# Moving the second convolution, the attention weights and the second Sinkhorn balancing of a fused convolution, attention and expert block

## The reference, cut to what matters

```python
x = x + _L0_conv_ref(_gn(x), ...)             # deformable convolution, 9 taps
# second layer, on g = _gn(x); x_l repeats g over n = 4 streams
x_norm = x_pooled * rsqrt(mean(x_pooled**2) + 1e-20) * rms_w
coeffs = x_norm @ phi_w.T + phi_b             # 24 numbers an image
H_pre  = sigmoid(alpha_pre * coeffs[:, :n]);  H_post = 2 * sigmoid(alpha_post * coeffs[:, n:2*n])
M = exp(alpha_res * coeffs[:, 2*n:].reshape(B, n, n))
for _ in range(20):                           # Sinkhorn: 40 half-steps
    M = M / sum(M, axis=-1, keepdims=True)
    M = M / sum(M, axis=-2, keepdims=True)
h_out = conv3x3(sum over streams of H_pre * x_l) + conv_b
x = x + mean(res_part + post_part, axis=1)    # res_part: diagonal of M times g; post_part: H_post times h_out
# third layer, on tokens t: 8 sequences of 256
t = t + attention(layernorm(t))               # 8 heads of 64, causal, softmax
# then two expert layers (8 experts top 2, 16 experts top 2) with a windowed sum between them
```

## Time and profile before

| what | value |
|---|---|
| median of 3 runs | 490.46 us |
| the profiled execution's own time | 486.73 us |
| its span, first to last instruction | 484.9 us |
| mean granted clock of TensorE | 0.982 |
| busy PE, DVE, ACT, POOL | 434.6, 347.4, 283.1, 175.6 us |
| end of the tap loop, last interpolation | 106.0 us |
| first exponential of attention | 139.05 us |
| first masks of steps 7, 16, 24, 33 | 154.89, 174.67, 194.13, 218.15 us |

### The profile page before, as it was taken

The page is one execution under the profiler, slowest core; times in us unless marked ns, Lnnn a source line. Parts: engine busy times, 40 slices in busy tenths (PEclk is TensorE's granted clock), DMA queues, the critical chain, the costliest instruction groups (busy, mean ns, idle before and its releaser), DMA issues.

```text
span 484.9 us, 9115 instructions
## 1 busy us (share of the span) xinstructions
PE 434.6 (90%) x2998; PEld 303.3 (63%) x2998; DVE 347.4 (72%) x1090; ACT 283.1 (58%) x676; POOL 175.6 (36%) x305
## 2 busy tenths in 40 slices
PE   2999999999968988979999988999989888998994
PEld 1787777767467887979898944344435444545542
DVE  4178998867777656788978853637666888797862
ACT  3467776732557876758788855765655333343431
POOL 4400001203134563383793342415341454343342
PEclk9998999999989998989999999999999999999998
DMA  7300000000400000012300004212112213041330
GB/s 178 144 2 1 2 0 1 1 2 0 87 3 1 1 2 1 2 39 51 69 20 3 1 3 141 63 39 68 43 38 74 68 45 105 28 122 66 99 102 11
DMA packets 13567, 20.94 MB, mean 43 GB/s; under 512 B 4592, under 2 KB 6384, under 8 KB 13008
## 3 DMA queue, kind: packets, MB, share of 16 engines
q1 hardware_dynamic: 13056, 19.99, 14.4%
q10 hardware_dynamic: 464, 0.37, 0.3%
HBM read 19.62 MB, written 0.72 MB: 42 GB/s over the span
## 4 chain that ended last, share of the span: by engine, by line
PE 63%; DVE 16%; ACT 8%; issue 6%; POOL 4%; DMA 2%; POOLq 0%; DVEq 0%; SPq 0%; ACTq 0%
PE PS L2171 14%; PE PS L1871 7%; PE PS L1909 6%; PE PS L2182 5%; PE PS L2193 5%; PE PS L1930 3%; PE PS L2103 3%; PE PS L2091 2%; PE PS L1829 2%; PE PS L1998 2%; PE PS L2013 2%; PE PS L2047 2%; ACT score_arena L968 2%; DVE QL L1468 2%; DVE score_arena L1577 2%
## 5 line engine op out<-in xcount | busy, mean ns | idle before, releaser
L2171 PE MATMUL PS<-YTs,WH 64*128 64x512 f32 x192 | 77.0, 427 | 1.9 <-ACT VV L1067 1.6
L735 POOL TENSOR_TENSOR pr<-pr 128x512 f32<-128x512 f32 x39 | 50.4, 1291 | 75.9 <-DVE pr L1630 44.7
L2171 PE MATMUL PS<-YX,WH 64*128 64x512 f32 x192 | 77.2, 426 | 0.0
L968 ACT ACTIVATE score_arena<-score_arena,nmx 128x128 f32<-128x128 f32 (+1 forms) x128 | 56.9, 446 | 22.2 <-DVE nmx L1577 21.8
L1067 ACT ACTIVATE VV<-PS 128x512 f32<-128x512 f32 x64 | 35.4, 595 | 41.6 <-PE PS L2171 41.5
L1023 ACT ACTIVATE stage<-PS,wk 128x512 f32<-128x512 f32 x64 | 40.8, 684 | 22.8 <-PE PS L2171 22.7
L1743 DVE TENSOR_TENSOR stage<-VV,PS 128x512 f32<-128x512 f32 x64 | 41.8, 682 | 17.1 <-ACT VV L1067 12.5
L2171 PEld LDWEIGHTS PS<-YTs,WH 64*128 64x128 f32 x192 | 35.3, 184 | 29.6 <-ACT VV L1067 12.6
L908 ACT ACTIVATE st_mem<-PS 128x512 f32<-128x512 f32 x72 | 37.3, 612 | 18.5 <-PE PS L1909 18.5
L2103 PE MATMUL PS<-cst,score_arena 128*128 128x128 f32 x192 | 34.4, 290 | 6.6 <-ACT score_arena L968 6.1
L2091 PE MATMUL PS<-YTs,QH 128*128 128x128 f32 (+1 forms) x128 | 38.9, 328 | 0.0
(11 more groups left out here) (277 smaller groups left out, 1130.1 us busy)
## 6 DMA issues: line engine op xcount, KB each, us to landing
QH<-gate_store SPq DMA_DIRECT2D x96, 128.0 KB, 2.9
stage<-in_wexp SPq DMA_DIRECT2D x6, 512.0 KB, 5.9
wk<-in_w SPq DMA_DIRECT2D x1, 1034.0 KB, 9.8
wa<-in_wat SPq DMA_DIRECT2D x1, 768.0 KB, 8.1
out<-X SPq DMA_DIRECT2D x16, 32.0 KB, 1.9
cst<-in_consts SPq DMA_DIRECT2D x1, 483.0 KB, 6.4
wc<-in_w SPq DMA_DIRECT2D x2, 183.5 KB, 5.8
score_arena<-in_wcv SPq DMA_DIRECT2D x2, 144.0 KB, 6.2
```

The lines of the kernel that those rows point to most:

```text
L735: nc.gpsimd.tensor_tensor(acc[:, c % 2], acc[:, c % 2], weighted[:, u % 2], ALU.add).then_inc(acc_added, 1)
L968: ins = nc.scalar.activation(PR[:, s % 3, cols], MS[:, s % 3, cols], ACT.Exp, bias=nmx[:, s % 3, qt:qt + 1], scale=-1.0, accum_out=rsum[:, ...
L2171: ins = mm(PS[:, banks[i], :], w[hs, m, tiles[i] * P:(tiles[i] + 1) * P], ys[i][hs, cs], start=(k == 0), stop=(k == 2))
```

## The change

Convolution 0 runs inside the tap loop, three taps after each of the steps 33, 34 and 35. Both convolutions accumulate in banks 5 and 6, and the attention weights in banks 1 to 4, so that batch 1's coefficients (now bank 4) and the gate spreads (now bank 7) move too. After the loop stand the gate spread of batch 0, the first pass of the weights, the group means and the diagonal spread, then the second pass with the first token transposes in its middle. Convolution 1 is cut in pieces: three taps before the transposes of yA, one after them, one after the first two projections, one after `scores(0)` and the other two projections, two in step 0 and one in step 1. All 40 half-steps of batch 1 run split between POOL and DVE in steps 0 to 21, two a step; its exponential moves to step 0 on ACT, its gates to step 0 on POOL and step 2 on DVE, and the spread of its gates becomes a fill of step 4 ("gS"), with ACT's bias in step 4 and DVE's convolution adds in step 5. DVE takes the middle reciprocal after both masks. The diagonal, the token transposes of tiles 2 and 3, their layer norms and one pair of folds move two or three steps later, and in image 3's steps the six projections move to steps 28 to 31.

```diff
-DIAG_AT, XT_AT, YA_AT = 18, (20, 27), (7, 25, 38)
-DVE_HALVES = 10
-POOL_HALVES = tuple(min(40, DVE_HALVES + 2 * s - (s > 3) - (s > 4)) for s in range(19))
-MID_INVERSE, END_INVERSE = [s for s in range(17) if s != 4], [s for s in range(15) if s != 3]
+DIAG_AT, XT_AT, YA_AT = 21, (22, 29), (7, 27, 38)
+DVE_HALVES = 0
+GATES_AT = 4
+POOL_HALVES = tuple(min(40, 2 * s) for s in range(21))
+MID_INVERSE, END_INVERSE = range(2, 22), range(1, 21)
...
-    return {0: (2, 3, 4, 5, 6, 7), 3: (2, 3, 4, 5, 6, 7)}.get(a, (0, 1, 2, 3, 4, 5))
+    return {0: (2, 3, 4, 5, 6, 7), 3: (4, 5, 5, 6, 6, 7)}.get(a, (0, 1, 2, 3, 4, 5))
...
+    if s == GATES_AT:
+        out.append(("gS", 0))
...
-HALVES = (8, 20, 25, 30, 36)
+HALVES = (6, 34, 38)
 PE_GROUP, PE_SQUARE, PE_COEF = 23, 26, 29
+CONV_AT = (33, 34, 35)
+CONV_SPLIT = (3, 4, 5)
+CONV_STEPS = (6, 8, 9)
 ACT_LOAD, ACT_NORM, ACT_EXP = 24, 26, 28
...
-                    if n == DVE_HALVES:
-                        pool.wait_ge(balanced, 2)
+                    if n == 0:
+                        pool.wait_ge(exp_ready, 2)
...
-            batch_gates(1)
...
+                if s == 0:
+                    batch_gates(1)
...
-                if s in (POWER_1, 21, 30):
-                    c = {POWER_1: 1, 21: 2, 30: 3}[s]
+                if s in (POWER_1, 23, 32):
+                    c = {POWER_1: 1, 23: 2, 32: 3}[s]
                     if c > 1:
                         add_proj_bias(c, {2: 3, 3: 5}[c])
                     ln_power(c)
-                for n in ((0, 1) if s == 19 else (a - 1,) if i == 1 and a > 2 else ()):
+                for n in ((0, 1) if s == 21 else (a - 1,) if i == 1 and a > 2 else ()):
...
             batch_apply(1)
-            batch_exp(1)
-            act.wait_ge(av_taken, 1)
-            copy_av(AVL, avl_ready)
             nc.scalar.activation(small[:, 40:40 + J], c_("euler"), ACT.Sqrt).then_inc(table_loaded, 1)
...
+            act.wait_ge(av_taken, 1)
+            copy_av(AVL, avl_ready)
...
             nc.scalar.activation(small[:, 44:44 + J], c_("euler"), ACT.Exp).then_inc(table_loaded, 1)
-            batch_bias(1)
...
                     act.wait_ge(masked_ready, s + 1)
+                    if s == 2:
+                        act.wait_ge(conv_ready, 2)
                     if s >= 3:
...
                 if s < STEPS:
+                    if s == GATES_AT:
+                        batch_bias(1)
                     for name in attention_fills(s):
...
+                if s == 0:
+                    batch_exp(1)
...
             copy_group(1)
-            half_steps(0, HALVES[2], HALVES[3])
-            copy_square(1)
-            half_steps(0, HALVES[3], HALVES[4])
-            copy_logits(1)
-            half_steps(0, HALVES[4], 2 * SINKHORN)
+            half_steps(0, HALVES[2], 2 * SINKHORN)
...
-                nc.vector.scalar_tensor_tensor(X1[:, j], PS[:, 1 + j // 2, (j % 2) * S:(j % 2 + 1) * S], CB[:, j, 1:2], X1[:, j],
+                nc.vector.scalar_tensor_tensor(X1[:, j], PS[:, 5 + j // 2, (j % 2) * S:(j % 2 + 1) * S], CB[:, j, 1:2], X1[:, j],
...
             second_residual(0)
-            half_steps(1, 0, 2)
-            gate_inverse(1)
             take_tokens(0)
             ln_center(0)
             ln_variance(0)
+            copy_square(1)
             ln_out(0, False)
             second_residual(1)
-            half_steps(1, 2, 4)
             ln_evac("yA", 0)
-            add_conv(2)
-            add_conv(3)
 
...
-            half_steps(1, 4, DVE_HALVES)
-            take_tokens(1)
...
+                nc.vector.tensor_tensor_reduce(MS[:, s % 3, P:3 * P], PS[:, s % 2, P:3 * P], c_("causal"), -SCALE, 1e30,
+                                               ALU.add, ALU.min, nmx[:, s % 3, 1:2]).then_inc(masked_ready, 1)
                 if s in MID_INVERSE:
                     inverse()
-                nc.vector.tensor_tensor_reduce(MS[:, s % 3, P:3 * P], PS[:, s % 2, P:3 * P], c_("causal"), -SCALE, 1e30,
-                                               ALU.add, ALU.min, nmx[:, s % 3, 1:2]).then_inc(masked_ready, 1)
                 if s >= 1:
                     take_fills(s - 1)
+                if s == 0:
+                    take_tokens(1)
+                    copy_logits(1)
+                if s == 2:
+                    gate_inverse(1)
+                if s == GATES_AT + 1:
+                    add_conv(2)
+                    add_conv(3)
                 if s == DIAG_AT + 1:
...
-                if s in (2, 21, 29):
-                    ln_center({2: 1, 21: 2, 29: 3}[s])
-                if s in (3, 22, 30):
-                    ln_variance({3: 1, 22: 2, 30: 3}[s])
-                if s in (5, 24, 32):
-                    ln_out({5: 1, 24: 2, 32: 3}[s], False)
+                if s in (2, 23, 31):
+                    ln_center({2: 1, 23: 2, 31: 3}[s])
+                if s in (3, 24, 32):
+                    ln_variance({3: 1, 24: 2, 32: 3}[s])
+                if s in (5, 26, 34):
+                    ln_out({5: 1, 26: 2, 34: 3}[s], False)
...
+            def conv(r, lo, hi):
+                pe.wait_ge(g2_ready, 2 * r + 2)
+                for k in range(lo, hi):
+                    ky, kx = divmod(k, 3)
+                    ins = mm(PS[:, 5 + r, :], w_conv[:, k, :], G2[r][:, :, ky:ky + HH, kx:kx + WW], start=(k == 0), stop=(k == TAPS - 1))
+                if hi == TAPS:
+                    ins.then_inc(conv_ready, 1)
...
+                if i in CONV_AT:
+                    if i == CONV_AT[0]:
+                        pe.wait_ge(conv_block_loaded, 32)
+                        pe.wait_ge(x1_tile_ready, 3)
+                    n = CONV_AT.index(i)
+                    conv(0, n * TAPS // len(CONV_AT), (n + 1) * TAPS // len(CONV_AT))
...
+            pe.wait_ge(v3_ready, 1)
+            mm(PS[:, 7, 32:36].rearrange("p (j k) -> p j k", k=2), spread, V3[0:B, 0, BATCHES[0], 1:3], start=True, stop=True).then_inc(cb_ready, 1)
...
+            query_weights(False)
+            value_weights(False).then_inc(av_ready, 1)
             pe.wait_ge(x1_tile_ready, J)
             group_means(1)
-            attention_weights(False).then_inc(av_ready, 1)
-            conv(0, 4, 5)
-            square_means(1)
-            conv(0, 5, TAPS)
-            coefficients(1)
-            pe.wait_ge(minus_ready, 1)
-            pe.wait_ge(avh_ready, 2)
-            attention_weights(True)
-            for n, (bank, width) in enumerate(((4, 512), (5, 512), (6, 256), (7, 256))):
-                at = 512 * n if n < 2 else 1024 + 256 * (n - 2)
-                ins = mm(PS[:, bank, 0:width], minus, AVH[:, at:at + width], start=False, stop=True)
-            ins.then_inc(av_taken, 1)
             pe.wait_ge(v3_diag_ready, 1)
             mm(PS[:, 0, 64:66], spread, V3[0:B, 0, BATCHES[0], 0], start=True, stop=True).then_inc(cb_diag_ready, 1)
...
-            conv(1, 0, 1)
...
-            transpose_x(0)
-            conv(1, 1, 6)
-            spread_gates(1)
-            conv(1, 6, 7)
-            transpose_y("yA", 0)
-            conv(1, 7, TAPS)
-            pe.wait_ge(avl_ready, 2)
-            pe.wait_ge(misc_free, FILL["yA", 0] + 1)
-            for name in FIRST_PROJECTIONS:
-                project(name)
-            transpose_x(1)
...
+            pe.wait_ge(avh_ready, 2)
+            query_weights(True)
+            transpose_x(0)
+            value_weights(True)
+            pe.wait_ge(minus_ready, 1)
+            for n, (bank, width) in enumerate(((1, 512), (2, 512), (3, 256), (4, 256))):
+                at = 512 * n if n < 2 else 1024 + 256 * (n - 2)
+                ins = mm(PS[:, bank, 0:width], minus, AVH[:, at:at + width], start=False, stop=True)
+            ins.then_inc(av_taken, 1)
+            square_means(1)
+            conv(1, 0, CONV_SPLIT[0])
+            transpose_y("yA", 0)
+            conv(1, CONV_SPLIT[0], CONV_SPLIT[1])
+            pe.wait_ge(avl_ready, 2)
+            pe.wait_ge(misc_free, FILL["yA", 0] + 1)
+            project(FIRST_PROJECTIONS[0])
+            project(FIRST_PROJECTIONS[1])
+            conv(1, CONV_SPLIT[1], CONV_SPLIT[2])
             scores(0)
+            project(FIRST_PROJECTIONS[2])
+            project(FIRST_PROJECTIONS[3])
+            coefficients(1)
+            conv(1, CONV_SPLIT[2], CONV_STEPS[0])
+            transpose_x(1)
...
+                if s < len(CONV_STEPS) - 1:
+                    conv(1, CONV_STEPS[s], CONV_STEPS[s + 1])
...
+                    if v == 4:
+                        pe.wait_ge(conv_added, J)
...
+                        elif what[0] == "gS":
+                            pe.wait_ge(v3_ready, 2)
+                            take(*what)
+                            mm(PS[:, 7, 0:4].rearrange("p (j k) -> p j k", k=2), spread, V3[0:B, 1, BATCHES[1], 1:3], start=True,
+                               stop=True).then_inc(misc_filled, 1)
```

(45 more changed lines are left out.)

19 lines of the change are left out of this document (10 added, 9 removed).

## The result

The changed kernel takes 498.22 us (median of 12 runs, 491.82 to 505.82) against 490.6 (12 runs, 487.87 to 495.42) for the kernel before: ratio 1.0115, interval 1.007 to 1.0161. It is slower by 1.2% by the ratio, some 5.6 us. The forecast was 492.0, +1.5 us: the sign is right, the size is not, and the median lies outside the range of 486.8 to 496.0.

The account below looks back on a forecast made before the run. TensorE carries 63% of the chain of waits, but DVE and the POOL-DVE balancing hold it in places. Terms -0.3, 0, 0, 0, +0.2 and +1.6 sum to +1.5 us: 492.0, range 486.8 to 496.0.

Parts of the forecast that it names:

- Convolution 0 in the loop hides nothing: Tap loop's end has no idle on PE, so nine taps take 8.0 us and move the last interpolation to 114.0.
- The new wait: After the loop PE waits from 117.2 to 119.2 for the first balancing's diagonal, idle for 2.0 us.
- The first exponential: At full clock it comes at 132.95 instead of 139.05, 6.1 us gained.
- Steps 0 to 6 give it back: They return 5.0 us of the front lead; 0.3 ahead remains, bounds 2.0 ahead to 1.5 behind.
- Steps 7 to 16: The same two half-steps a step as before, so 0.
- Steps 16 to 24: Bank 7's wait goes but POOL's fold delays step 23: 19.5 us, sum 0, bounds -2.5 and +1.5.
- Rival 2: Not slower: waits of steps 19 to 24 really go, 487.9 at full clock, 489.5 with half clock; chance 0.32.
- Step 29: PE waits some 2.7 us for DVE before the image transpose; steps 24 to 34 sum 0, bounds -1.5 and +2.5.
- rival 3: Crowding of steps 28 to 31 costs its upper bound, half clock after step 29: +2.5, 494.5; chance 0.12.
- Behind step 34: After 218 nothing is edited and PE is busy 62.65 of 65.85 us, so a lead or lag stays.
- The clock: After the new idle the clock halves, 3.2 us of PE work shrinking to 1.6: +1.6, bounds 0 and 1.6.
- Rival 1: Clock stays full after the new wait: sum -0.1, no change, 490.4; chance 0.22.

Follow-up runs that it names:

- e3: Changed kernel with all nine taps of convolution 0 moved out of the tap loop, in front of the first diagonal; 492.59 us, ratio 1.000.
- e1: Changed kernel with two convolution taps of idle work filling TensorE's wait for the first diagonal; 495.36 us, ratio 1.0119.
- e11: e2 with filler matmuls at six later idles (steps 3, 4, 7, 21, 25, 29); 485.51 us, ratio 0.9892 to the kernel before.
- e5: Changed kernel with four TensorE idles filled by unread matmuls (first diagonal, steps 3, 21 and 29); 492.15 us, ratio 1.0022.
- e4: Changed kernel with image 4's projections at steps 28, 29, 30, 30, 31, 31; 497.68 us, ratio 1.0154.
- e9: e5 without the filler at the first diagonal, so the new wait stands alone; 497.05 us, ratio 1.0134.
- e8: Changed kernel with convolution 0's last three taps behind the first diagonal's spread instead of in the loop; 501.74 us, ratio 1.0129.
- e10: e8 with filler matmuls at the three later idles (steps 3, 21 and 29); 493.06 us, ratio 1.0076.
- e6: Kernel before with filler matmuls at its own four idles (steps 0, 1, 20 and 30); 487.15 us, ratio 0.9925.
- e2: Changed kernel with convolution 0's last three taps moved from the loop into the wait for the first diagonal; 493.3 us, ratio 0.999.
- e12: Changed kernel run again as it is, for a second trace; 498.23 us, ratio 1.0117.

## Why the prediction was wrong, by its steps

*Convolution 0 in the loop hides nothing*: right (e3). *The new wait*: right, 117.33 to 119.17, 1.84 us against 2.0. *The first exponential*: right at full clock, 133.39 in e1 against 132.95 (the prediction's own terms add up to 132.7). *Steps 0 to 6 give it back*: right. From 0.83 ahead at the first mask to 4.80 behind at step 7's is 5.6 us, and at full clock, in e11, these steps take 21.97 us against 16.74 before (at a clock of 0.90), 5.2 lost where the forecast, from 6.1 ahead to 0.3, has 5.8.

```profile
128.20:150.17 21.97, 21.65 (x156) 18.44 (x155) 13.50 (x59) 14.45 (x48) 9.14 (x40) 1.00 0.04 9
```

POOL's gates are read from the first line below, five operations to 147.5; DVE's next reciprocal waits for the half-step behind them, masks step 3 only at 148.50, and PE idles for 1.95 us until 150.22.

```profile
146.01 0.19 POOL L633 TENSOR_TENSOR gs<-ef 8x4 f32<-8x4 f32 x1 [0.40 <-DVE ef L1307]
...
147.38 0.19 POOL L641 TENSOR_TENSOR V<-V,cst 8x8 f32<-8x8 f32 x1
```

*Steps 7 to 16*: 19.02 us against 19.78 before. *Steps 16 to 24*: 19.57 us against 19.5 forecast, with the wait on the fold at the normalisation 6.4 us behind the last reciprocal (6.1 forecast). Rival 2 falls with it. One thing was missed there: the second diagonal comes from POOL late enough to hold PE for 1.32 us at step 21.

```profile
190.41 0.17 DVE L1333 RECIPROCAL mn<-mn 8x4 f32<-8x4 f32 x1 [0.27 <-POOL mn L652]
...
196.86 0.69 DVE L1500 TENSOR_TENSOR pr<-PS,rinv 128x512 f32<-128x512 f32 x1 [0.66 <-POOL T L725]
```

*Step 29*: PE waits 2.60 us, 2.7 forecast. But steps 24 to 34 take 30.47 us against 25.56, +4.9 where the bound was +2.5: the wait is followed by 13.8 us at half clock, the one it replaced by 3.2. The crowding itself costs nothing, 25.02 us at full clock in e11; the prediction had the half clock behind this wait only in rival 3, at half of what it took. *Behind step 34* nothing is edited, but a lead there does not always stay, as the sum took it to: from step 63's first mask to the end it is 209.8 us before and 209.7 in the changed kernel, but 213.9 in e1, e5 and e11, each with three stretches of 3.4 us at half clock there.

*The clock* is the step that failed. The prediction set +1.6 for it with bounds 0 and 1.6, from stretches of 3.2 us. It asked whether the clock would fall and took the length of the fall for a constant. Measured, the stretch behind the new wait is 13.2 to 13.4 us in three traces of this order and 10.1 in e4, and costs 4.9 us (e9 against e5); the loss as a whole rose by 6.6. Two things made the sample a poor one. The profiled execution of before was a lucky one (8.7 lost, mean 12.4). And the lengths vary between executions: 3.2 and 9.8 us near the same wait of step 3, 3.4 to 13.5 behind that of step 21. That the thin products keep the stretch behind the new wait long each time is what e8 and e10 speak for, without proving it. So the sign came out by the term that the prediction named, the clock; its size did not.

Rival 1 went by the idle of 2.10 us before 362.46, which left the clock up. That idle comes back in all 14 traces: in seven a half clock of 3.4 us begins at it or less than 1 us behind, in seven none does. So one row could not tell either way. The new wait had the half clock in all six traces that have it.

The Trainium skill (TensorE: Matmul & The Clock Gate, HAM oscillation) tells of a kernel whose waits of some 3 to 5 us throttle the array each time, so that the work behind them starts cold. The waits here are shorter, 1.83 to 2.77 us at the first diagonal, and yet the work behind them started at half clock in five of six traces, in e4 0.9 us later.

## What to carry to other kernels

Price a new wait on TensorE by the stretch behind it and not by the idle alone: the half clock over the thin products behind it cost 4.9 us, 2.7 times the idle of 1.84. So keep movable dense work (here taps) in front of the point where the queue may run dry, or else first behind it. An idle of 1 to 2 us can be worth filling even with matmuls that compute nothing (0.7% in e6), but judge it with the other idles filled as well, since the loss can turn up elsewhere. And look at each run's granted clock before comparing two orders: a single profile can be the lucky one, and one stretch at half clock says little about the length of the next.

## What the runs showed of the hardware

The half clock held for 13.4 us although PE had no gap in that stretch, and for 7.0 (of which 5.5 beside PE's work) when taps came first. Attention work ran at half clock for as long, 13.5 us in e2 with PE busy for 13.41 of them. All 12 runs of the changed kernel lost between 15.2 and 30.7 us to it, runs of the kernel before between 8.7 and 17.7, and in each kernel the run time followed. The Trainium skill (TensorE: Matmul & The Clock Gate, Part 1: The HAM clock gate (the "warmup" mystery)) says that the number of slow matmuls differs between runs of one kernel; the stretches at half clock do so here (behind step 21's wait 6.8 us in the changed kernel's first trace, 3.4 in e12's).
